# A hybrid layer kernel: attention without a loop and with two accumulators, early first loads, and a product of the delta layer on GpSimd

## The chip, the cores and the metric

The kernel runs on one core of a Trainium2 chip. The metric is the device time of one execution in microseconds, the median over several runs. A profiled execution gives the busy times, waits and timelines that are quoted here.

## What is computed

Four layers are added to a residual x of 4 x 1024 tokens and 128 channels: attention a, a mixture of experts, a gated delta layer b, and the same mixture of experts again. Cut to what matters here:

```python
# attention a, 16 heads of 8 channels
cov  = einsum('bhqd,bhkd->bhqk', q - mean(q), k - mean(k)) / d
attn = softmax(cov + q_var * k_var / d)
x    = x + (attn @ v) @ Wo.T
# delta layer b, per batch and head, state S of 8x8, over time t
S_new = a_t*S - a_t*b_t*(S k_t) k_t' + b_t * v_t k_t'
o_t   = q_t S_new
x     = x + O @ Wo.T + bo
```

## The kernel before, in words

The kernel is a chain of blocks in the order of `build`; each block gives every engine its own program, and engines meet through semaphores.

**Projection** (`project_qkv`, lines 264 to 433). The tokens go through in eight chunks of 512. TensorE projects q, k and v, ScalarE and VectorE split q and k into three bf16 parts, and SP stores these parts and those of the variances to DRAM (`scr.terms`, lines 424 and 428), four DMAs a chunk. The buffers of parts alternate between two. GpSimd clears the operand tiles `g.q_op` and `g.k_op` first (lines 311 and 315).

**Attention** (`attend`, from line 443). A unit is one batch and one group of four heads; there are 16 units, numbered u = 4b + s. SP loads the operands of a group, 3 DMAs for k and 9 for q, with `load` (lines 524 and 528). TensorE makes two kinds of score. Those for the maxima (line 567) are reduced by VectorE (line 696) over 1024 keys. The maxima are turned (line 621), split in three parts (lines 707 to 714), and written as rows of the operand. Those for the probabilities (line 582) come out transposed with the maxima already taken off; ScalarE takes their exponential (line 684). TensorE multiplies the exponentials with v into `ps_acc` (line 599). A unit has 32 steps. In a step TensorE issues two halves of maximum scores for a later unit, two probability scores and one product with v, all written out in this order in `body`. Both kinds of score have two PSUM buffers. After each half of the queries (16 steps) the accumulator is handed over: ScalarE copies `ps_acc` to SBUF in two parts (line 667, at places 7 and 8 of the exponentials, `COPY_AT`), TensorE turns the copy with four products against the identity (line 611) into `ps_misc`, and VectorE normalises from there (lines 719 and 725, one reciprocal and four multiplications). As there is one `ps_acc`, the product with v skips a step at the hand-over, and two are made in the next. `ps_misc` also takes the turned maxima. `batches` makes batch 0 and batch 3 straight code and runs batches 1 and 2 in a loop, on every engine. Groups of v are staged by GpSimd (line 511), one copy a unit.

The output projection, the expert layer, a convolution and the solve of the delta layer follow.

**Output part of the delta layer** (`delta_out`, from line 1861). For each of four batches and eight rows e of the state: TensorE spreads k (line 1934), VectorE multiplies it with u (line 2008), scans over time (line 2029) and multiplies the states with q (line 2035), and TensorE adds the result up (line 1944). The tiles `kd`, `St` and `qS` have two buffers each. After row 3, VectorE also adds the previous batch's output to x and takes its statistics (line 2015, `add`). GpSimd has only clearing to do in this block.

## Time and profile before

| | |
|---|---|
| median of three runs | 2043.8 us (2043.46 to 2047.93) |
| profiled execution | 2043.38 us, its span 2041.7 us |
| projection | 21 to 92 us |
| attention | 92 to 912 us |
| output projection, experts | 913 to 1160 us |
| delta layer's output part | 1633 to 1815 us |
| experts again | 1815 to 2041.7 us |
| VectorE busy | 1540.1 us (75%) |
| TensorE matmul busy | 1361.8 us (67%) |
| ScalarE busy | 917.1 us (45%) |
| GpSimd busy | 227.3 us (11%) |

Times in a timeline count from the start of the span. Busy time of matmuls is modelled: matmuls overlap, so the distance from one start to the next tells the pace, and the length of one does not. A line of a timeline may merge several instructions of one kind (x4). The words behind a left arrow name what ended the idle time before the instruction. PEclk is the share of full clock that TensorE was granted.

### The profile page before, as it was taken

To read this page: it belongs to the slowest core of one execution; us is meant where nothing else is said; L and a number is where in the kernel's file an instruction comes from. 1 tells how busy PE (TensorE), PEld (TensorE's weight loads), DVE (VectorE), ACT (ScalarE), POOL (GpSimd) and SP (SyncE) were. 2 spreads that over 40 slices of the span, in tenths; PEclk is the share of its full clock that TensorE was granted. 3 is DMA by queue.
4 is the path that set the end of the run, shared out by engine and by line. 5 is a ranking of instruction groups with operands and counts; after the bars stand their busy time and mean duration, and the time that the engine had idled before them with its cause. 6 is when DMAs were issued, how large, how long until landed. Compare 5 with 4: busy or idle time off the path is not lost. (4 is left out here: it accounts for less than half of the span.)

```text
span 2041.7 us, 44670 instructions
## 1 busy us (share of the span) xinstructions
PE 1361.8 (67%) x15216; PEld 723.2 (35%) x15216; DVE 1540.1 (75%) x3117; ACT 917.1 (45%) x2009; POOL 227.3 (11%) x218
## 2 busy tenths in 40 slices
PE   4489999999999999984399674000000078841998
PEld 2214444444444444443166442000000024420665
DVE  5598888888788888707166576899999899972665
ACT  4507777777677777774143273001222200030343
POOL 6000000000000000003414300000000000025044
PEclk9858999999999999997699876555555589965999
DMA  3430111111111110003224415810222010012243
GB/s 98 120 80 5 40 41 30 29 29 29 30 29 29 29 29 3 3 20 96 60 55 66 75 67 117 212 41 10 63 63 54 19 41 0 0 43 58 55 67 44
DMA packets 118670, 101.05 MB, mean 49 GB/s; under 512 B 23665, under 2 KB 100018, under 8 KB 118066
## 3 DMA queue, kind: packets, MB, share of 16 engines
q1 hardware_dynamic: 101570, 84.79, 16.2%
q0 software_dynamic: 11264, 8.92, 3.0%
q10 hardware_dynamic: 5616, 4.47, 1.3%
q8 instruction: 130, 2.13, 0.4%
q14 instruction: 90, 0.74, 0.1%
HBM read 55.98 MB, written 31.21 MB: 43 GB/s over the span
## 5 line engine op out<-in xcount | busy, mean ns | idle before, releaser
L696 DVE TENSOR_REDUCE att_negmax<-att_ps_max 128x1 f32<-128x1024 f32 x512 | 613.9, 1221 | 112.5 <-PE att_ps_max L567 91.8
L684 ACT ACTIVATE att_probs<-att_ps_prob 128x512 f32<-128x512 f32 x1024 | 561.4, 598 | 244.7 <-PE att_ps_prob L582 233.8
L567 PE MATMUL att_ps_max<-av_k_op,av_q_op 81*32 81x512 bf16 x4096 | 418.0, 404 | 43.1 <-DMA av_q_op<-terms_q 18.9
L582 PE MATMUL att_ps_prob<-av_q_op,av_k_op 99*32 99x512 bf16 x4096 | 406.9, 385 | 9.2 <-ACT att_probs L684 1.2
L599 PE MATMUL att_ps_acc<-att_probs,att_vq 128*32 128x256 f32 x4096 | 308.3, 381 | 0.0
L1926 PE MATMUL out_ps_y<-all_bo_row,all_ones 1*128 1x128 f32 x2 | 0.8, 482 | 372.8 <-PEq L104 372.8
L567 PEld LDWEIGHTS att_ps_max<-av_k_op,av_q_op 81*32 81x32 bf16 x4096 | 109.4, 98 | 184.2 <-DVE att_negmax L696 80.6
L582 PEld LDWEIGHTS att_ps_prob<-av_q_op,av_k_op 99*32 99x32 bf16 x4096 | 108.1, 95 | 174.1 <-ACT att_probs L684 129.7
L599 PEld LDWEIGHTS att_ps_acc<-att_probs,att_vq 128*32 128x32 f32 x4096 | 126.4, 111 | 82.3 <-issue 5.8
L1145 ACT ACTIVATE moe_moe_gate<-moe_moe_ps_h 128x256 f32<-128x256 f32 x122 | 46.8, 383 | 214.2 <-PE moe_moe_ps_h L1086 214.2
L1926 PEld LDWEIGHTS out_ps_y<-all_bo_row,all_ones 1*128 1x128 f32 x2 | 0.5, 305 | 373.1 <-issue 373.1
L1086 PE MATMUL moe_moe_ps_h<-all_w_all,moe_moe_xgT 128*128 x244 | 128.0, 607 | 1.4 <-DVE moe_moe_xgT L1286 1.4
L1310 DVE TENSOR_TENSOR moe_moe_y<-moe_moe_y,moe_moe_ps_y 128x128 f32 x182 | 52.4, 288 | 89.3 <-issue 81.0
L1835 ACT ACTIVATE solve_p<-solve_state,solve_decay 128x32 f32<-128x32 f32 x128 | 45.0, 351 | 155.7 <-DVE solve_state L1819 155.7
L1101 PE MATMUL moe_moe_ps_y<-all_w_all,moe_moe_hT 128*128 x728 | 111.6, 276 | 0.3
L1101 PEld LDWEIGHTS moe_moe_ps_y<-all_w_all,moe_moe_hT 128*128 128x128 f32 x728 | 95.7, 192 | 1.5 <-issue 1.5
L1286 DVE COPY moe_moe_xgT<-moe_moe_ps_g 128x256 f32<-128x256 f32 x92 | 38.2, 415 | 69.4 <-PE moe_moe_ps_g L1079 69.4
L511 POOL COPY att_vq<-av_v 128x288 f32<-128x288 f32 (+1 forms) x16 | 6.8, 427 | 728.6 <-PE att_ps_acc L599 728.5
L1079 PE MATMUL moe_moe_ps_g<-all_ident,moe_moe_xin 128*128 128x128 f32 x182 | 36.5, 280 | 69.8 <-DMA moe_moe_xin<-expert_rows 69.6
L1944 PE MATMUL out_ps_o<-out_qS,out_gather 128*128 128x512 f32 x128 | 65.0, 632 | 25.8 <-DVE out_qS L2035 25.7
L1302 DVE SCALAR_TENSOR_TENSOR moe_moe_hs<-moe_moe_gate,moe_moe_scale,moe_moe_ps_h 128x256 f32<-128x256 f32 x122 | 58.3, 478 | 20.2 <-ACT moe_moe_gate L1145 20.0
L2029 DVE TENSOR_TENSOR_SCAN out_St<-b_a,out_kd 128x1024 f32<-128x1024 f32 x32 | 73.1, 2284 | 0.4
(277 smaller groups left out, 2067.4 us busy)
## 6 DMA issues: line engine op xcount, KB each, us to landing
moe_moe_xin<-expert_rows SPq DMA_DIRECT2D x182, 72.0 KB, 1.8
av_k_op<-terms_k SPq DMA_DIRECT2D x48, 216.0 KB
av_q_op<-terms_q SPq DMA_DIRECT2D x144, 72.0 KB
solve_dec_and_windows<-solve_Xw SPq DMA_DIRECT2D x16, 256.0 KB, 3.0
solve_dec_and_windows<-solve_k SPq DMA_DIRECT2D x16, 256.0 KB, 3.7
terms_q<-qkv_parts_q SPq DMA_DIRECT2D x8, 384.0 KB, 2.6
terms_k<-qkv_parts_k SPq DMA_DIRECT2D x8, 384.0 KB, 3.2
all_w_all<-in_f_w SPq DMA_DIRECT2D x24, 128.0 KB, 2.5
```

The costliest lines, as they stand in the source:

```text
L567: mm = pe.matmul(ps_max[c * STRIP:(c + 1) * STRIP, a % 2, k * CH:(k + 1) * CH], q_op[s][0:R_ALL, h, at:at + STRIP], k_op[s][0:R_ALL, h, k ...
L582: mm = pe.matmul(ps_prob[c * STRIP:(c + 1) * STRIP, j % 2, :], k_op[s][0:R_END, h, at:at + STRIP], q_op[s][0:R_END, h, half * CH:(half + 1 ...
L599: mm = pe.matmul(ps_acc[32 * h:32 * h + 32, cols], vq[:, s % 2, kt, VW * h:VW * h + 32], probs[:, (GH * v + h) % PROBS, cols], start=(kt = ...
L684: act.activation(probs[:, j % PROBS, :], ps_prob[:, j % 2, :], ACT.Exp).then_inc(s_exp, 1)
L696: dve.tensor_reduce(negmax[:, s % 2, a:a + 1], ps_max[:, a % 2, :], AX.X, ALU.max, negate=True).then_inc(s_maxed, 1)
L1086: pe.matmul(ps_up[n % 3][:, :, :].rearrange("p w f -> p (w f)"), xgT[:, n // 2 % 3, cols], wall[:, bass.ds(at0, 2 * F)], start=True, stop= ...
L1101: mm = pe.matmul(ps_y[n % 2][:, 0:P], hT[:, n % 3, i * P:(i + 1) * P], wall[:, bass.ds(at0 + (2 * F + i * P), P)], start=(i == 0), stop=(i ...
L1145: act.activation(gate[:, n % 3, :], ps_up[n % 3][:, 0, :], ACT.Silu).then_inc(s_silu, 1)
L1302: dve.scalar_tensor_tensor(out=hs[:, n % 3, :], in0=gate[:, n % 3, :], scalar=scale[:, n:n + 1], in1=ps_up[n % 3][:, 1, :], op0=ALU.mult, ...
L1310: dve.tensor_tensor(tile, tile, ps_y[n % 2][:, 0:P], ALU.add).then_inc(s_sum, 1)
L1944: mm = pe.matmul(ps_o[:, i * CH:(i + 1) * CH], gather[:, e, :, :].rearrange("p h d -> p (h d)"), qS[:, e % 2, i * CH:(i + 1) * CH], start= ...
L2029: dve.tensor_tensor_scan(St[:, e % 2, :], a[:, tok], kd[:, e % 2, :], 0.0, ALU.mult, ALU.add).then_inc(s_S, 1)
```

## The change

Four things are changed.

1. The operands of the first two head groups of batch 0 are loaded by SP inside the projection, two sets (of one DMA for k and three for q) after each of the chunks 2, 3 and 4, once the first two chunks are stored and the operand tiles cleared. The loop over chunks on SP is written out.
2. All four batches of attention are straight code on every engine.
3. There are two accumulators in PSUM, one for each half of the queries, and no `ps_misc`. The copied accumulator is turned by four transposes back into its own accumulator's bank, and VectorE normalises from there with one reciprocal and one multiplication. The turned maxima go to the first accumulator. The product with v comes in every step. It waits at the start of a half for the last reader of that bank, and no longer for the copy of the other half. The copies come at places 6 and 8.
4. In the delta layer's output part the product of q with the states is made by GpSimd. VectorE's scan waits for the product two before.

```diff
@@ -416,25 +416,48 @@
 
         @block.sync
         def _(sp):
-            def body(i):
-                for p in range(2):
-                    at = (2 * i + p) * CH
-                    for w in range(2):
-                        sp.wait_ge(s_p3[w][p], i + 1)
-                        sp.dma_start(scr.terms[w][:, 0:D, :, bass.ds(at, CH)].rearrange("i d h t -> (d h) i t"),
-                                     parts[w][:, p, :, :]).then_inc(s_out[p], 16)
-                    sp.wait_ge(s_v3[p], i + 1)
-                    for w in range(2):
-                        sp.dma_start(scr.terms[w][:, D, :, bass.ds(at, CH)].rearrange("i h t -> h i t"),
-                                     vparts[32 * w:32 * w + H, p, :, :]).then_inc(s_out[p], 16)
-            repeat(sp, NC_ // 2, body)
+            def store(c):
+                i, p = c // 2, c % 2
+                tok = slice(c * CH, (c + 1) * CH)
+                for w in range(2):
+                    sp.wait_ge(s_p3[w][p], i + 1)
+                    sp.dma_start(scr.terms[w][:, 0:D, :, tok].rearrange("i d h t -> (d h) i t"),
+                                 parts[w][:, p, :, :]).then_inc(s_out[p], 16)
+                sp.wait_ge(s_v3[p], i + 1)
+                for w in range(2):
+                    sp.dma_start(scr.terms[w][:, D, :, tok].rearrange("i h t -> h i t"),
+                                 vparts[32 * w:32 * w + H, p, :, :]).then_inc(s_out[p], 16)
+
+            early = [(s, i) for s in range(EARLY) for i in range(NPART)]
+            for c in range(NC_):
+                store(c)
+                if c == 2:
+                    for p in range(2):
+                        sp.wait_ge(s_out[p], 16 * NDMA)
+                    sp.wait_ge(s_ones, 1 + 3 * NQ)
+                if c >= 2:
+                    for s, i in early[2 * (c - 2):2 * (c - 1)]:
+                        load_terms(sp, g, scr, 0, s, i)
             for p in range(2):
                 sp.wait_ge(s_out[p], 16 * NDMA * (NC_ // 2))
 
 
+EARLY = 2
+
+
+def load_terms(sp, g, scr, b, s, i):
+
+    heads, tok, row = slice(s * GH, (s + 1) * GH), slice(b * S, (b + 1) * S), i * NPART * K1
+    sp.dma_start(g.k_op[s][row:row + NPART * K1, :, :],
+                 scr.terms[1][:, :, heads, tok].rearrange("j d h t -> (j d) h t")).then_inc(g.s_load[s], 16)
+    for j in range(NPART):
+        sp.dma_start(g.q_op[s][row + j * K1:row + (j + 1) * K1, :, :],
+                     scr.terms[0][i, :, heads, tok]).then_inc(g.s_load[s], 16)
+
+
 LEAD = 8
 PV_LAG = 3
-COPY_AT = 2 * PV_LAG + 1
+COPY_AT = 2 * PV_LAG
 PROBS = 16
 STEPS = GH * TB
...
-        ps_acc = m.ps("ps_acc", [P, CH])
-        ps_misc = m.ps("ps_misc", [P, CH])
-        comb = ps_misc[:, P:P + CT * GH * VW].rearrange("p (t g r) -> p t g r", t=CT, g=GH)
...
-        def batches(eng, body):
-
-            body(0, True, False)
-            with eng.Fori(1, last_b) as b:
-                body(b, False, False)
-            body(last_b, False, True)
+        def batches(body):
+
...
-                                 ).then_inc(s_load[s], 16)
-                    for j in range(NPART):
-                        sp.dma_start(q_op[s][row + j * K1:row + (j + 1) * K1, :, :],
-                                     scr.terms[0][i, :, heads, tok]).then_inc(s_load[s], 16)
+                    load_terms(sp, g, scr, b, s, i)
 
...
-            for s in range(NQ):
+            for s in range(EARLY, NQ):
                 load(0, s)
...
-                        pe.wait_ge(s_acc, 2 * u + half)
+                    if kt == 0:
+                        read = max(1, 3 * u) if half == 0 else 3 * u + 1
+                        pe.wait_ge(s_misc, read)
 
                 for h in range(GH):
-                    mm = pe.matmul(ps_acc[32 * h:32 * h + 32, cols], vq[:, s % 2, kt, VW * h:VW * h + 32],
+                    mm = pe.matmul(ps_acc[half][32 * h:32 * h + 32, cols], vq[:, s % 2, kt, VW * h:VW * h + 32],
                                    probs[:, (GH * v + h) % PROBS, cols], start=(kt == 0 and part == 0),
                                    stop=(kt == TB - 1 and part == 1))
                 mm.then_inc(s_pv, 1)
 
-            def combine(b, s, half, last=False):
+            def combine(b, s, half):
 
                 u = NQ * b + s
                 pe.wait_ge(s_acc, 2 * u + half + 1)
-
-                pe.wait_ge(s_misc, 3 * u + 1 + 2 * half - last)
                 for t in range(CT):
-                    mm = pe.matmul(comb[:, t], acc_sb[:, half, t * P:(t + 1) * P],
-                                   g.ident[:, :].rearrange("p (g r) -> p g r", g=GH)[:, :, 0:VW],
-                                   start=True, stop=True)
+                    mm = pe.transpose(ps_acc[half][:, t * P:(t + 1) * P], acc_sb[:, half, t * P:(t + 1) * P],
+                                      g.ident[:, :])
                 mm.then_inc(s_comb, 1)
 
             def turn_max(b, s):
                 u = NQ * b + s
                 pe.wait_ge(s_maxed, STEPS * (u + 1))
-                if not (isinstance(b, int) and b == 0 and s == 0):
+                if not (b == 0 and s == 0):
                     pe.wait_ge(s_misc, 3 * u - 1)
-                pe.transpose(ps_misc[0:STEPS, 0:P], negmax[:, s % 2, :], g.ident[:, :]).then_inc(s_nmT, 1)
+                pe.transpose(ps_acc[0][0:STEPS, 0:P], negmax[:, s % 2, :], g.ident[:, :]).then_inc(s_nmT, 1)
 
             for a in range(STEPS):
...
                             scores_for_prob(b, s, 2 * i + half)
                         w = i - PV_LAG
-
-                        for w in (w - 1, w) if w % (2 * TB) == 1 else () if w % (2 * TB) == 0 else (w,):
-                            if w >= 0:
-                                pv(b, s, w // 2, w % 2)
-                            elif not (first and s == 0):
-                                pv(*prev(b, s), (w + STEPS) // 2, w % 2)
+                        if w >= 0:
+                            pv(b, s, w // 2, w % 2)
+                        elif not (first and s == 0):
+                            pv(*prev(b, s), (w + STEPS) // 2, w % 2)
                         if i == PV_LAG + 1 and not (first and s == 0):
                             combine(*prev(b, s), 1)
                         if i == STEPS // 2 + PV_LAG + 1:
                             combine(b, s, 0)
                         if i == STEPS - LEAD + 1 and not (last and s == NQ - 1):
                             turn_max(*nxt(b, s, 1))
-            batches(pe, body)
+            batches(body)
             for w in range(STEPS - PV_LAG, STEPS):
                 pv(last_b, NQ - 1, w // 2, w % 2)
-            combine(last_b, NQ - 1, 1, last=True)
+            combine(last_b, NQ - 1, 1)
 
         @block.scalar
         def _(act):
...
-                    if not (isinstance(b, int) and b == 0 and s == 0):
+                    if not (b == 0 and s == 0):
                         act.wait_ge(s_comb, 2 * u + half - 1)
                 cols = slice(part * CH // 2, (part + 1) * CH // 2)
-                ins = act.activation(acc_sb[:, half, cols], ps_acc[:, cols], ACT.Copy)
+                ins = act.activation(acc_sb[:, half, cols], ps_acc[half][:, cols], ACT.Copy)
                 if part == 1:
                     ins.then_inc(s_acc, 1)
...
-                            copy_acc(*prev(b, s), 1, j - COPY_AT)
-                        if STEPS + COPY_AT <= j <= STEPS + COPY_AT + 1:
-                            copy_acc(b, s, 0, j - STEPS - COPY_AT)
+                        if j in (COPY_AT, COPY_AT + 2) and not (first and s == 0):
+                            copy_acc(*prev(b, s), 1, (j - COPY_AT) // 2)
+                        if j in (STEPS + COPY_AT, STEPS + COPY_AT + 2):
+                            copy_acc(b, s, 0, (j - STEPS - COPY_AT) // 2)
                         act.wait_ge(s_prob, 2 * STEPS * u + j + 1)
                         if j % GH == 0 and not (first and s == 0 and j < PROBS):
 
                             act.wait_ge(s_pv, 4 * TB * u + 2 * ((j - PROBS) // GH + 1))
                         act.activation(probs[:, j % PROBS, :], ps_prob[:, j % 2, :], ACT.Exp).then_inc(s_exp, 1)
-            batches(act, body)
...
                 chain.done(dve.tensor_copy(parts[:, 0, :], rows))
                 chain.done(dve.tensor_tensor(rest, rows, parts[:, 0, :], ALU.subtract))
...
-                dve.reciprocal(rsum[:, half, :, :], comb[:, :, :, D]).then_inc(s_rsum, 1)
+                dve.reciprocal(rsum[:, half, :, :], comb[half][:, :, :, D]).then_inc(s_rsum, 1)
                 dve.wait_ge(s_rsum, 2 * u + half + 1)
-                for t in range(CT):
-                    tile = b * TB + half * CT + t
-                    out = g.o[:, bass.ds(tile, 1), s * GH * D:(s + 1) * GH * D].rearrange(
-                        "p o (g d) -> p (o g) d", g=GH)
-                    ins = dve.tensor_tensor(out, comb[:, t, :, 0:D],
-                                            rsum[:, half, t, :].unsqueeze(2).to_broadcast([P, GH, D]), ALU.mult)
-                ins.then_inc(s_misc, 1)
+                tile = b * TB + half * CT
+                out = g.o[:, tile:tile + CT, s * GH * D:(s + 1) * GH * D].rearrange("p t (g d) -> p t g d", g=GH)
+                dve.tensor_tensor(out, comb[half][:, :, :, 0:D],
+                                  rsum[:, half, :, :].unsqueeze(3).to_broadcast([P, CT, GH, D]),
+                                  ALU.mult).then_inc(s_misc, 1)
 
             for a in range(STEPS):
...
@@ -1921,6 +1925,14 @@
             pool.wait_ge(s_same, 3)
             pool.memset(gather[:, :, :, :], 0.0).then_inc(s_same, 1)
 
+            for b in range(B):
+                for e in range(D):
+                    n = D * b + e
+                    pool.wait_ge(s_S, n + 1)
+                    wait_used(pool, s_o, n - 1)
+                    pool.tensor_tensor(qS[:, e % 2, :], q[:, b * S:(b + 1) * S], St[:, e % 2, :],
+                                       ALU.mult).then_inc(s_qS, 1)
+
         @block.tensor
         def _(pe):
             pe.matmul(ps_y[0][:, 0, :], g.ones[0:1, :], g.bo_row[:, :], start=True, stop=True).then_inc(s_bo, 1)
@@ -2020,22 +2032,20 @@
                 for t in range(TB):
                     bn_stats_of(nc, g, b * TB + t)
 
-            def body(b):
-                tok = bass.ds(b * S, S)
+            for b in range(B):
+                tok = slice(b * S, (b + 1) * S)
                 spread_u(b, 0)
                 for e in range(D):
                     n = D * b + e
                     dve.wait_ge(s_kd, n + 1)
+                    wait_used(dve, s_qS, n - 1)
                     dve.tensor_tensor_scan(St[:, e % 2, :], a[:, tok], kd[:, e % 2, :], 0.0, ALU.mult,
                                            ALU.add).then_inc(s_S, 1)
                     if e < D - 1:
+                        dve.wait_ge(s_S, n)
                         spread_u(b, e + 1)
-                    dve.wait_ge(s_S, n + 1)
-                    wait_used(dve, s_o, n - 1)
-                    dve.tensor_tensor(qS[:, e % 2, :], q[:, tok], St[:, e % 2, :], ALU.mult).then_inc(s_qS, 1)
-                    if e == 3 and not (isinstance(b, int) and b == 0):
+                    if e == 3 and b:
                         add(b - 1)
-            repeat(dve, B, body)
             add(B - 1)
 
         @block.scalar
```

## Rows read from the trace of the kernel before

**Rows 1.** Busy time by stretch: stretch, length, then busy us per engine, PEclk, DMA.
```profile
253.00:300.00 47.00, 45.85 (x797) 22.64 (x788) 40.84 (x49) 35.72 (x69) 0.43 (x1) 1.00 0.14 32
```

**Rows 2.** Timeline of GpSimd in attention: start us, length us, engine, line, operation.
```profile
206.94 0.43 POOL L511 COPY att_vq<-av_v 128x288 f32<-128x288 f32 x1 [112.77 <-PE att_ps_acc L599]
...
347.72 0.43 POOL L511 COPY att_vq<-av_v 128x288 f32 x1 [46.46 <-PE att_ps_acc L599]
...
734.41 0.43 POOL L511 COPY att_vq<-av_v 128x288 f32<-128x288 f32 x1 [47.14 <-PE att_ps_acc L599]
...
828.24 0.43 POOL L511 COPY att_vq<-av_v 128x288 f32<-128x288 f32 x1 [46.49 <-PE att_ps_acc L599]
```

**Rows 3.** Timeline of TensorE matmuls round one hand-over of the accumulator.
```profile
300.42 0.39 PE L567 MATMUL att_ps_max<-av_k_op,av_q_op 81*32 81x512 bf16 x4
...
303.87 1.08 PE L611 MATMUL att_ps_misc<-all_ident,att_acc_sb 128*128 128x36 f32 x8
...
304.88 0.40 PE L567 MATMUL att_ps_max<-av_k_op,av_q_op 81*32 81x512 bf16 x4
...
306.19 0.39 PE L567 MATMUL att_ps_max<-av_k_op,av_q_op 81*32 81x512 bf16 x4
```

**Rows 4.** Timeline of TensorE in the output projection: four transposes, then the next four.
```profile
923.81 0.60 PE L809 MATMUL oproj_ps_t<-all_ident,a_o 128*128 128x128 f32 x4
...
924.25 0.60 PE L824 MATMUL oproj_ps_x<-all_ident,all_x 128*128 128x128 f32 x4
```

**Rows 5.** Timeline of ScalarE in attention: an accumulator copy, a pair of exponentials.
```profile
302.31 0.41 ACT L667 ACTIVATE att_acc_sb<-att_ps_acc 128x256 f32<-128x256 f32 x1
...
308.16 1.09 ACT L684 ACTIVATE att_probs<-att_ps_prob 128x512 f32<-128x512 f32 x2 [0.22 <-PE att_ps_prob L582]
```

**Rows 6.** Timeline of all engines, from the projection to the first score.
```profile
37.15 14.20 POOL L315 MEMSET av_k_op<- 3x4096 bf16 x4
...
51.48 0.39 SPq L428 DMA_DIRECT2D terms_k<-qkv_vparts  x1
...
92.25 0.29 SPq L524 DMA_DIRECT2D av_k_op<-terms_k  x1
...
103.80 1.90 PE L567 MATMUL att_ps_max<-av_k_op,av_q_op 81*32 81x512 bf16 x16 [18.86 <-DMA av_q_op<-terms_q]
```

**Rows 7.** Busy time by stretch: the delta layer's output part.
```profile
1645.00:1803.00 158.00, 131.82 (x373) 60.37 (x371) 154.34 (x144) 7.27 (x16) 0.00 (x0) 0.98 0.00 0
```

**Rows 8.** Timeline of VectorE in the delta layer's output part.
```profile
1645.51 1.22 DVE L2008 TENSOR_TENSOR out_kd<-out_u,out_ps_k 128x1024 f32<-128x1024 f32 x1 [3.97 <-PE out_ps_k L1934]
...
1646.76 2.29 DVE L2029 TENSOR_TENSOR_SCAN out_St<-b_a,out_kd 128x1024 f32<-128x1024 f32 x1
...
1664.56 2.28 DVE L2029 TENSOR_TENSOR_SCAN out_St<-b_a,out_kd 128x1024 f32<-128x1024 f32 x1
...
1666.77 1.19 DVE L2008 TENSOR_TENSOR out_kd<-out_u,out_ps_k 128x1024 f32<-128x1024 f32 x1
...
1669.01 2.28 DVE L2029 TENSOR_TENSOR_SCAN out_St<-b_a,out_kd 128x1024 f32<-128x1024 f32 x1
...
1799.61 1.23 DVE L2035 TENSOR_TENSOR out_qS<-b_q,out_St 128x1024 f32<-128x1024 f32 x1
```

**Rows 9.** GpSimd's groups by line and shape: busy us, mean ns, idle before.
```profile
L511 POOL COPY att_vq<-av_v 128x288 f32<-128x288 f32 x8 | 3.4, 427 | 346.3 <-PE att_ps_acc L599 346.2
```

**Rows 10.** Timeline of VectorE and of GpSimd at the start of the expert layer.
```profile
957.37 1.08 DVE L1241 TENSOR_TENSOR moe_moe_lower<-moe_moe_base,moe_moe_first 128x896 f32<-128x896 f32 x1
...
957.90 1.60 POOL L1055 DMA_INDIRECT expert_rows<-moe_moe_xr,moe_moe_slot  x1 [11.30 <-ACT moe_moe_xr L1135]
...
962.83 0.97 POOL L1055 DMA_INDIRECT expert_rows<-moe_moe_xr,moe_moe_slot  x1 [0.30 <-issue]
...
964.03 0.69 DVE L1251 TENSOR_TENSOR_SCAN moe_moe_upto<-moe_moe_unit,moe_moe_needed 128x256 f32<-128x256 f32 x1
...
964.10 1.39 POOL L1055 DMA_INDIRECT expert_rows<-moe_moe_xr,moe_moe_slot  x1 [0.30 <-issue]
```

More of the change, by code:

```diff
@@ L461, in attend @@
         ps_prob = m.ps("ps_prob", [P, 2, CH])
-        ps_acc = m.ps("ps_acc", [P, CH])
-        ps_misc = m.ps("ps_misc", [P, CH])
-        comb = ps_misc[:, P:P + CT * GH * VW].rearrange("p (t g r) -> p t g r", t=CT, g=GH)
+        ps_acc = [m.ps(f"ps_acc{half}", [P, CH]) for half in range(2)]
+        comb = [a[:, :].rearrange("p (t g r) -> p t g r", t=CT, g=GH) for a in ps_acc]
         s_clear = m.sem("cleared")
-        s_load = m.sems("loaded", NQ)
         s_scored = m.sem("scored")
@@ L577, in scores_for_prob @@
                     pe.wait_ge(s_nmrow, 16 * NPART * (u + 1))
-                if not (isinstance(b, int) and b == 0 and s == 0 and j < 2):
+                if not (b == 0 and s == 0 and j < 2):
                     pe.wait_ge(s_exp, 2 * STEPS * u + j - 1)
@@ L693, in reduce_max @@
                 dve.wait_ge(s_scored, STEPS * u + a + 1)
-                if a == 0 and not (isinstance(b, int) and b == 0 and s < 2):
+                if a == 0 and not (b == 0 and s < 2):
                     dve.wait_ge(s_nmT, u - 1)
@@ L702, in split_max @@
                 dve.wait_ge(s_nmT, u + 1)
-                if not (isinstance(b, int) and b == 0 and s < 2):
+                if not (b == 0 and s < 2):
                     dve.wait_ge(s_nmrow, 16 * NPART * (u - 1))
@@ L706, in split_max @@
                 rows, rest, parts = nm_rows[:, :], nm_rest[:, :], nm_parts[:, s % 2]
-                ins = dve.tensor_copy(rows, ps_misc[0:STEPS, 0:P])
+                ins = dve.tensor_copy(rows, ps_acc[0][0:STEPS, 0:P])
                 ins.then_inc(s_misc, 1)
-                dve.wait_ge(s_misc, 1 if isinstance(u, int) and u == 0 else 3 * u)
+                dve.wait_ge(s_misc, max(1, 3 * u))
                 chain.done(dve.tensor_copy(parts[:, 0, :], rows))
@@ L2021, in add @@
                     bn_stats_of(nc, g, b * TB + t)
-            def body(b):
-                tok = bass.ds(b * S, S)
+            for b in range(B):
+                tok = slice(b * S, (b + 1) * S)
                 spread_u(b, 0)
```

19 lines of the change are left out of this document (8 added, 11 removed).

## The prediction

> **What bounds the kernel now.** I read the busy time by stretch first, then the timelines of GpSimd, of TensorE and of VectorE where the change reaches. One attention unit (a batch and a group of four heads, of which there are 16) has TensorE busy for 45.85 of 47.0 us at granted clock 1.00, and VectorE for 40.84 [rows 1]. So TensorE is the bound there, and VectorE is close enough to stop it at times. The copies of v on GpSimd mark the units, since each waits for the products of an earlier unit: three static units take 140.78 us (46.93 each), the two last 93.83 us (46.92 each), but the eight intervals that touch the loop take 386.69 us (48.34 each) [rows 2]. Inside a unit an ordinary step of TensorE takes 304.88 to 306.19, 1.31 us, while the two steps from 300.42 to 304.88, in which the accumulator changes hands, take 4.46 us: 1.84 us beyond two ordinary steps, of which 1.01 is the combining product [rows 3]. In the output part of the delta layer VectorE is busy for 154.34 of 158.0 us and TensorE for 131.82 [rows 7]. There VectorE is the bound, one step (products with k, scan, product with q) taking 1664.56 to 1669.01, 4.45 us [rows 8].
>
> **Part 1, early loads.** The first score waits until 103.80, though the attention block's queue starts at 92.25 [rows 6]. The change issues the operands of head groups 0 and 1 in the projection, 2 load sets (8 DMAs) after each of chunks 2, 3 and 4. SP is moved past two things. One is the wait for GpSimd's memsets, which end at 37.15 + 14.20 = 51.35, before chunk 2's last store is issued at 51.48 [rows 6], so I cost it at nothing. The other is the stores of chunks 3 to 5, each queued behind 8 issues of 0.3 to 0.4 us (the block's first is 0.29), some 3 us of a chunk of 8 (eight chunks from 21 to 92 us, less the first one's start); what hides this is that parts buffers are wanted again only two chunks later, and if the cover goes, up to 3 us for each of three chunks are lost. TensorE can begin some 0.02 us behind the block's first issue, so the gain is 103.80 - 92.27 = **11.5 us**. What is late next is VectorE's own chain of maxima, which simply starts earlier; groups 2 and 3 are still loaded in the block and are not wanted for over 50 us.
>
> **Part 2, no loop in attention.** All four batches become straight code for all five engines. Batches 0 and 3 are already that, so their pace is the measure: 386.69 - 8 x 46.92 = **11.3 us**. The bounds of this term are 0 (if the longer code has to be fetched at a cost that batches 0 and 3 don't show) and 11.3; I take 11.3, since the static rows are the same code.
>
> **Part 3, the hand-over of the accumulator.** There are 31 hand-overs that something waits for: one in the first unit, two in each of the fifteen others (the very last counts below). Three things shrink each. The combining product becomes four transposes; the nearest rows have four transposes 128x128 f32 issued in 923.81 to 924.25, 0.44 us [rows 4], in place of 1.01. Two PSUM buffers take away the reason for skipping one step of the probability-value product and doing two in the next. The ScalarE copies go to places 6 and 8 of the exponentials instead of 7 and 8; each takes 0.4 us, and a pair of exponentials 1.09 [rows 5], so two steps ask 1.5 us of ScalarE where TensorE has 1.31 and then 1.31 plus the transposes. I work out that the second exponential of the first such step ends at 1.9 us from that step's start, and TensorE wants its buffer at 1.96 less a latency of some 0.2: a wait of 0.1 to 0.2, plus 0.1 on switching to the transposes. New excess: 0.44 + 0.3 = 0.75 against 1.84, a gain of 1.09 x 31 = **33.8 us**. Bounds: 1.4 each (0.44 alone, 43 us) and 0.57 each (only the shorter combine, 18 us). The added waits on the readers of the PSUM buffers (normalise, split of the maxima) stand three or more steps behind those readers and cost nothing; if they did, scores and products queued behind them on TensorE, and ScalarE after them, would stop. Normalise becomes one multiplication instead of four; it mostly overlaps, and with the shorter end of the last unit I give it **2 us**. Attention together: 11.5 + 11.3 + 33.8 + 2 = **58.6 us less**.
>
> **Part 4, the product with q on GpSimd.** It takes 1.23 us from each of 32 steps of VectorE [rows 8] and adds 32 products of 128x1024 on GpSimd, with a wait for the scan ahead of each, and a wait of each scan for the product two before. Behind GpSimd's wait nothing else is queued; who waits for it is TensorE's sum and, two steps on, the scan. No row shows such a product. The nearest is a one-input copy of 288 columns in 0.427 us [rows 9]; with 0.1 for the start that is 1.15 ns a column, so 1024 columns take 1.3 us if a second input is free and 2.4 to 2.5 if it costs as much as the first. I take 2.3, near the upper end, because both inputs have to be read. The Trainium skill (GPSIMD Engine Reference, section 3.1) gives 4497 ns for 2048 columns of a two-input add; half of it, 2.25, would change the sum by 1.6 us.
>
> Whether this overlaps the scan decides the part. The trace has GpSimd instructions that read SBUF while VectorE works. Behind a VectorE multiply or scan with two SBUF inputs they last longer: 1.60 us, begun 0.55 us before such an instruction ended, and 1.39 us, begun just as a scan started; between the two, with no such instruction beside it, one takes 0.97 [rows 10]. So GpSimd is held while such a VectorE instruction runs, and the scan is one. Then in each step scan and product exclude one another: 2.28 + 0.1 (semaphore) + 2.3 + 0.1 (release) = 4.78 us, in place of 4.45. This holds whichever of the two yields. The rows show only GpSimd yielding. The Trainium skill (SBUF — State Buffer, section Who interferes with whom) says the first to start keeps the shared ports for its whole instruction and the other blocks fully, either way round; no row shows the reverse. By that rule and its 2.25 the part would cost some 6 us, and with no such rule it would gain 21.
>
> Sum for the stage, from the first product at 1645.51. Before: it ends at 1799.61 + 1.23, 155.3 us. That is 1.25 (1645.51 to 1646.76) + 31 x 4.45 + three adds + the last scan and product, 3.5, and leaves 4.2 us for each add. After: 1.25 + 31 x 4.78 = 149.4; three adds at 4.2 less the 1.3 us that VectorE now idles in a step, 8.7; the last scan and product 4.7; together 162.8. So **7.5 us more**. The vector engine's saving of 39 us goes into its wait for GpSimd.
>
> **The sum.** The profiled execution took 2043.4 us (span 2041.7 and 1.7 around it), 0.4 under the median of 2043.8. 2043.4 - 58.6 + 7.5 = 1992.3; I forecast **1992.5 us**.
>
> **Rivals.**
> (a) Scan and product overlap. Then VectorE's step is 1.25 + 2.21 (1664.56 to 1666.77) = 3.45 us and it needs 1.25 + 31 x 3.45 + 12.6 + 4.7 = 125.5 us and TensorE, with 131.8 busy [rows 7] and little idle left, becomes the bound at about 134: 21 us less instead of 7.5 more, in all 2043.4 - 58.6 - 21 = **1964 us**. For it: the delayed GpSimd rows are DMA issues, not arithmetic. Against it: their delays follow the ends of the two-input VectorE instructions.
> (b) The hand-over gains only the shorter combine, because ScalarE's copies or VectorE's split of the maxima become what TensorE waits for (VectorE has 40.84 of 47.0 us already [rows 1]): 33.8 falls to 18, **2008 us**. For it: only two buffers lie between each pair of engines.
> (c) The change doesn't do what it says: the loads don't land early, or they hold up the stores, and the 11.5 us come back: **2004 us**. Against it: DMA has room between the stores.
> (d) Slower than before: GpSimd's product is far slower than the copy's rate says. Every 1 us beyond 2.3 costs 32 us, so from about 3.9 us a product (2.3 + 51/32) the whole is slower; at 4.5 us it is 1992.3 + 70 = **2063 us**. Against it: that would be 3.8 times the copy's time for a column.
>
> **Chances.** Forecast 0.66, (a) 0.19, (b) 0.07, (c) 0.04, (d) 0.04. A measurement of this kernel can tell about 0.2% (4 us) from no change. Faster by over that: all but (d) and a sliver, 0.95; within it 0.01; slower 0.04. The range reaches down past (a) to 1960, since a fifth lies there, and up to 2003, for a product of 2.46 us (5 more) and part of (b). Around the forecast alone it would be 1982 to 2001.
>
> **What would show it.** First score at about 92.3. Units of 44.7 us, all alike, with hand-overs of 3.3 to 3.4 us for two steps, and no idle gap of TensorE in mid-attention. In the delta output, scans 4.8 us apart with VectorE idle 1.3 us in each step, released by GpSimd, and GpSimd busy nearly half of the stage with products that begin at a scan's end. Scans about 4 us apart and TensorE without gaps would prove (a); a product that starts and goes on while a scan runs, both at their lengths, disproves the exclusion. A product over 3 us, units above 46 us, or a first score after 100 us would make the forecast wrong.

## The result and the profile after

The changed kernel takes 1984.35 us (median of four runs, 1981.33 to 1986.57); the kernel before 2043.63 us (2041.33 to 2047.93). The ratio is 0.9707, with a 95% interval of 0.9685 to 0.9728. The profiled execution took 1985.79 us, its span 1984.1 us, which is 57.6 us less than the one of before.

Where these 57.6 us went, by the starts of the blocks: attention ends 62.4 us earlier (the expert layer starts at 876.42 instead of 938.80). From there to the delta layer's output part it takes 697.3 us instead of 694.5, and the last expert layer 228.6 instead of 226.6. Nothing is changed in these two stretches; in the other kernels below, where they are the same code, they take 693.8 to 700.6 and 226.0 to 227.7, so I count the 4.8 us as scatter, though 228.6 lies 0.9 us above what any other kernel shows. The output part takes 181.80 us instead of 181.78.

**Attention.** First the start, in the timelines of SP's queue and of TensorE (start, duration, engine, line, operation, output <- input, count; in brackets the idle time before and what ended it):

```profile
51.82 0.43 SPq L428 DMA_DIRECT2D terms_k<-qkv_vparts  x1
52.37 0.27 SPq L451 DMA_DIRECT2D av_k_op<-terms_k  x1
52.68 1.06 SPq L454 DMA_DIRECT2D av_q_op<-terms_q  x3
...
70.70 1.00 SPq L454 DMA_DIRECT2D av_q_op<-terms_q  x3
```
```profile
92.72 1.90 PE L577 MATMUL att_ps_max<-av_k_op,av_q_op 81*32 81x512 bf16 x16 [7.23 <-PEq L104]
```

The first score starts at 92.72 instead of 103.80 [rows 6], and it no longer waits for a DMA (PEq is TensorE's own sequencer). Then the units, by GpSimd's copies of v, where the loop used to be:

```profile
415.65 0.43 POOL L530 COPY att_vq<-av_v 128x288 f32<-128x288 f32 x1 [44.09 <-PE att_ps_acc L610]
460.24 0.43 POOL L530 COPY att_vq<-av_v 128x288 f32<-128x288 f32 x1 [44.16 <-PE att_ps_acc L610]
504.79 0.43 POOL L530 COPY att_vq<-av_v 128x288 f32<-128x288 f32 x1 [44.12 <-PE att_ps_acc L610]
549.37 0.43 POOL L530 COPY att_vq<-av_v 128x288 f32<-128x288 f32 x1 [44.16 <-PE att_ps_acc L610]
```

All 13 intervals are 44.50 to 44.65 us, where [rows 2] had 46.92 outside of the loop and 48.34 at it. One hand-over on TensorE:

```profile
482.38 0.65 PE L610 MATMUL att_ps_acc<-att_probs,att_vq 128*32 128x256 f32 x8
482.81 0.43 PE L577 MATMUL att_ps_max<-av_k_op,av_q_op 81*32 81x512 bf16 x4
483.03 0.44 PE L592 MATMUL att_ps_prob<-av_q_op,av_k_op 99*32 99x512 bf16 x4
483.25 0.44 PE L577 MATMUL att_ps_max<-av_k_op,av_q_op 81*32 81x512 bf16 x4
483.47 0.44 PE L592 MATMUL att_ps_prob<-av_q_op,av_k_op 99*32 99x512 bf16 x4
483.70 0.65 PE L610 MATMUL att_ps_acc<-att_probs,att_vq 128*32 128x256 f32 x8
484.28 0.66 PE L620 MATMUL att_ps_acc<-all_ident,att_acc_sb 128*128 128x128 f32 x4
484.87 0.40 PE L577 MATMUL att_ps_max<-av_k_op,av_q_op 81*32 81x512 bf16 x4
```

An ordinary step is 1.31 us; this one is 482.81 to 484.87, 2.06, so the excess is 0.75 instead of 1.84 [rows 3]. The transposes are issued 0.15 us later than the pace would have them (484.28 instead of 484.13), and the next score 0.59 behind them.

**The delta layer's output part.** Timelines of VectorE and GpSimd, and the groups of the block (count | busy us, mean ns | idle before and its releaser):

```profile
1593.96 1.19 DVE L2020 TENSOR_TENSOR out_kd<-out_u,out_ps_k 128x1024 f32<-128x1024 f32 x1
1595.18 3.44 DVE L2042 TENSOR_TENSOR_SCAN out_St<-b_a,out_kd 128x1024 f32<-128x1024 f32 x1
1598.54 1.19 DVE L2020 TENSOR_TENSOR out_kd<-out_u,out_ps_k 128x1024 f32<-128x1024 f32 x1
1599.77 3.44 DVE L2042 TENSOR_TENSOR_SCAN out_St<-b_a,out_kd 128x1024 f32<-128x1024 f32 x1
...
1594.12 2.35 POOL L1933 TENSOR_TENSOR out_qS<-b_q,out_St 128x1024 f32<-128x1024 f32 x1 [2.23 <-DVE out_St L2042]
1598.70 2.36 POOL L1933 TENSOR_TENSOR out_qS<-b_q,out_St 128x1024 f32<-128x1024 f32 x1 [2.23 <-DVE out_St L2042]
```
```profile
L2042 DVE TENSOR_TENSOR_SCAN out_St<-b_a,out_kd 128x1024 f32<-128x1024 f32 x32 | 105.2, 3288 | 1.0
L2020 DVE TENSOR_TENSOR out_kd<-out_u,out_ps_k 128x1024 f32<-128x1024 f32 x32 | 38.1, 1191 | 4.0 <-PE out_ps_k L1946 4.0
...
L1933 POOL TENSOR_TENSOR out_qS<-b_q,out_St 128x1024 f32<-128x1024 f32 x32 | 75.3, 2353 | 90.1 <-DVE out_St L2042 90.1
```

The product takes 2.353 us. The scan, 2.28 us before [rows 8], is now recorded with a mean of 3.288: 28 of the 32 take some 3.44, and the first of all and the one behind each of the three `add`, which have no product beside them, take 2.27 to 2.29. The one shown begins at 1595.18, while the product of 1594.12 runs (until 1596.47), and ends at 1598.62, 2.15 us behind the product's end. The next product starts 0.08 us later. A step is 4.58 us. The product with k (1598.54 to 1599.73) has one input in PSUM, lies beside a product on GpSimd (from 1598.70), and neither is longer for it. VectorE is busy by the records nearly as long as before and has hardly any idle time: its wait is inside the scan.

### The profile page after: what moved, and what is told of

It reads as the page before. It is cut to its first block and busy times, and to the rows that moved or that the text cites. A ratio compares the mean times of both kernels' runs of the same rounds, so it can differ in the third digit from the quotient of the medians.

```text
span 1984.1 us, 42351 instructions
## 1 busy us (share of the span) xinstructions
PE 1330.6 (67%) x15088; PEld 724.9 (37%) x15088; DVE 1533.5 (77%) x2989; ACT 916.6 (46%) x2009; POOL 302.3 (15%) x250
## 5 line engine op out<-in xcount | busy, mean ns | idle before, releaser
L577 PE MATMUL att_ps_max<-av_k_op,av_q_op 81*32 81x512 bf16 x4096 | 420.5, 401 | 24.4 <-DVE att_negmax L702 15.5
L610 PE MATMUL att_ps_acc<-att_probs,att_vq 128*32 128x256 f32 x4096 | 314.8, 379 | 0.0
L577 PEld LDWEIGHTS att_ps_max<-av_k_op,av_q_op 81*32 81x32 bf16 x4096 | 114.5, 97 | 160.5 <-DVE att_negmax L702 62.8
L610 PEld LDWEIGHTS att_ps_acc<-att_probs,att_vq 128*32 128x32 f32 x4096 | 133.3, 111 | 76.5 <-issue 0.5
L530 POOL COPY att_vq<-av_v 128x288 f32<-128x288 f32 x16 | 6.8, 427 | 672.0 <-PE att_ps_acc L610 671.9
L2042 DVE TENSOR_TENSOR_SCAN out_St<-b_a,out_kd 128x1024 f32<-128x1024 f32 x32 | 105.2, 3288 | 1.0
L1933 POOL TENSOR_TENSOR out_qS<-b_q,out_St 128x1024 f32<-128x1024 f32 x32 | 75.3, 2353 | 90.1 <-DVE out_St L2042 90.1
```

The lines of the kernel that those rows point to most:

```text
L577: mm = pe.matmul(ps_max[c * STRIP:(c + 1) * STRIP, a % 2, k * CH:(k + 1) * CH], q_op[s][0:R_ALL, h, at:at + STRIP], k_op[s][0:R_ALL, h, k ...
L610: mm = pe.matmul(ps_acc[half][32 * h:32 * h + 32, cols], vq[:, s % 2, kt, VW * h:VW * h + 32], probs[:, (GH * v + h) % PROBS, cols], start ...
L1933: pool.tensor_tensor(qS[:, e % 2, :], q[:, b * S:(b + 1) * S], St[:, e % 2, :], ALU.mult).then_inc(s_qS, 1)
L2042: dve.tensor_tensor_scan(St[:, e % 2, :], a[:, tok], kd[:, e % 2, :], 0.0, ALU.mult, ALU.add).then_inc(s_S, 1)
```

## The experiments

The experiments ran in three rounds on three chips, each beside the kernel before, which took 2043.77 to 2045.55 us there. The ratios allow for that; of two times from different rounds, a difference of 2 us says nothing, as the kernel before alone moved by 1.8.

### Product back on VectorE

```diff
-                    pool.tensor_tensor(qS[:, e % 2, :], q[:, b * S:(b + 1) * S], St[:, e % 2, :],
-                                       ALU.mult).then_inc(s_qS, 1)
...
-                    wait_used(dve, s_qS, n - 1)
...
+                    dve.wait_ge(s_S, n + 1)
+                    wait_used(dve, s_o, n - 1)
+                    dve.tensor_tensor(qS[:, e % 2, :], q[:, tok], St[:, e % 2, :], ALU.mult).then_inc(s_qS, 1)
```

> The changed kernel with the product of q with the states back on VectorE, everything else as changed. If the product on GpSimd and the scan exclude one another (a step of 4.58 us in place of 4.45, but 1.2 us less behind each add), the output part takes 155 us either way and the whole stays at 1984, within 3 us. If the product on GpSimd had cost the 7.5 us that was forecast, this kernel would take 1977. If it had gained anything by overlap, this kernel would take more than 1990.

Measured: 1981.94 us, ratio to before 0.9695 (0.9679 to 0.9711), against 0.9707 (0.9685 to 0.9728) with the product on GpSimd. The block takes 181.2 us, a step 4.45. So moving the product is worth nothing that can be measured: the intervals overlap, the block differs by 0.6 us, and the 59 us come from attention.

### The scan's second input from PSUM

```diff
-                wait_used(pe, s_kd, n - 1)
+                wait_used(pe, s_S, n - 1)
...
-                dve.tensor_tensor(kd[:, e % 2, :], u[:, bass.ds(b * S, S)], ps_k[e % 2][:, :],
+                dve.tensor_tensor(ps_k[e % 2][:, :], u[:, bass.ds(b * S, S)], ps_k[e % 2][:, :],
...
-                    dve.tensor_tensor_scan(St[:, e % 2, :], a[:, tok], kd[:, e % 2, :], 0.0, ALU.mult,
+                    dve.tensor_tensor_scan(St[:, e % 2, :], a[:, tok], ps_k[e % 2][:, :], 0.0, ALU.mult,
```

> The changed kernel with the products u times k written back into their PSUM tile, so that the scan has one input in SBUF and one in PSUM; TensorE waits for the scan before it overwrites the tile. Exclusion by the two SBUF inputs: scan and product run beside one another, the scan is recorded at 2.3 us again, a step falls from 4.58 to 3.5 to 4.1 us with TensorE as the bound, the output part from 155 to about 134 us, the whole to about 1963. Exclusion of any VectorE work by GpSimd, or a cost of the waits alone: the step stays at 4.5 us or more and the whole at 1984.

Measured: 1961.88 us (1958.44 to 1962.68), ratio to before 0.959 (0.9574 to 0.9606), 22.5 us below the changed kernel and 20.1 below the product on VectorE. The block takes 157.4 us, 24.4 less than in the changed kernel. Its timelines of VectorE and GpSimd:

```profile
1593.15 2.29 DVE L2041 TENSOR_TENSOR_SCAN out_St<-b_a,out_ps_k 128x1024 f32<-128x1024 f32 x1
1595.36 1.21 DVE L2019 TENSOR_TENSOR out_ps_k<-out_u,out_ps_k 128x1024 f32<-128x1024 f32 x1
1596.60 2.29 DVE L2041 TENSOR_TENSOR_SCAN out_St<-b_a,out_ps_k 128x1024 f32<-128x1024 f32 x1
...
1595.52 2.35 POOL L1932 TENSOR_TENSOR out_qS<-b_q,out_St 128x1024 f32<-128x1024 f32 x1 [1.09 <-DVE out_St L2041]
```

The product runs from 1595.52 to 1597.87 and the scan starts in the middle of it, at 1596.60; both have their own length. A step is 3.45 us. This is what rival (a) of the prediction described, and its 1964 us is 2 us off. It had TensorE as the bound at 134 us; in fact VectorE sets most steps, and waits for TensorE's products with k for 10.7 us in all, 4.0 in the changed kernel. Only the place of one tile has changed, which the product with k writes and the scan reads, and with it what TensorE waits for before it overwrites that tile. The product with k ran free beside GpSimd already when it wrote to SBUF, so the exclusion belongs to the scan with two SBUF inputs.

### The control: the same scan, product on VectorE

The diff is that of the two experiments above, taken together.

> A control for the experiment in which the scan reads its second input from PSUM: the same scan and the same PSUM buffer, but the product with q on VectorE as in the kernel before. If that experiment's gain came from overlap with GpSimd alone, a step takes 1.17 + 2.28 + 1.23 less the overlaps of one instruction's start with the one before = 4.45 us as before and the time is 1983 us, within 3. If reading from PSUM makes the scan or the product with k faster by itself, the step is below 4.3 us and the time below 1979 us.

Measured: 1985.20 us, ratio 0.9717 (0.9698 to 0.9736), a step again 4.45 us with the scan at 2.280. PSUM makes nothing faster by itself. The 20 to 24 us need both: the product on GpSimd, and a scan that leaves GpSimd alone.

### The product made twice

GpSimd makes each product twice; nobody reads the first.

```diff
+                    pool.tensor_tensor(qS[:, 2 + e % 2, :], q[:, b * S:(b + 1) * S], St[:, e % 2, :], ALU.mult)
                     pool.tensor_tensor(qS[:, e % 2, :], q[:, b * S:(b + 1) * S], St[:, e % 2, :],
```

> The changed kernel with each product on GpSimd made twice, the first into a tile that nobody reads. Exclusion: a step becomes 2.23 + 2 x 2.35 = 6.9 us, the output part 31 x 2.35 + 2 = 75 us longer, the whole about 2059. If scan and product may overlap and only GpSimd's own time counts, a step is 4.8 us and the whole about 1991.

Measured: one run of 2043.38 us; the block takes 242.1 us, 60 more, and a step 6.60. Far from what overlap would give, but 16 us below the 2059 that I wrote. The timelines of VectorE and GpSimd say why:

```profile
1602.32 4.36 DVE L2043 TENSOR_TENSOR_SCAN out_St<-b_a,out_kd 128x1024 f32<-128x1024 f32 x1
...
1602.18 2.35 POOL L1933 TENSOR_TENSOR out_qS<-b_q,out_St 128x1024 f32<-128x1024 f32 x1
1604.49 4.33 POOL L1934 TENSOR_TENSOR out_qS<-b_q,out_St 128x1024 f32<-128x1024 f32 x1
1608.78 2.35 POOL L1933 TENSOR_TENSOR out_qS<-b_q,out_St 128x1024 f32<-128x1024 f32 x1
```

The scan waits from 1602.32 for the first product, which ends at 1604.53. It goes before the second product, and ends at 1606.68, 2.15 us later. The second product, recorded from 1604.49, ends 2.14 us after the scan. So here GpSimd is held by VectorE, and one of its instructions is recorded at 4.33 us instead of 2.35. The exclusion works in both directions, and a scan that waits goes in between two products that are both ready. Only the head of a held instruction is free: the second product costs 2.14 us, not 2.35, and 31 x (6.60 - 4.58) is 63 us. The block shows 60; 4 of the 32 second products were not held, and I did not follow the last 3 us further.

### Three buffers for the states and the products

```diff
-        St = m.sb("St", [P, 2, S])
-        qS = m.sb("qS", [P, 2, S])
+        St = m.sb("St", [P, 3, S])
+        qS = m.sb("qS", [P, 3, S])
...
-                    wait_used(dve, s_qS, n - 1)
-                    dve.tensor_tensor_scan(St[:, e % 2, :], a[:, tok], kd[:, e % 2, :], 0.0, ALU.mult,
+                    wait_used(dve, s_qS, n - 2)
+                    dve.tensor_tensor_scan(St[:, n % 3, :], a[:, tok], kd[:, e % 2, :], 0.0, ALU.mult,
```

> The changed kernel with three buffers for the states and for their products with q in place of two, and the waits one buffer further back. Exclusion: nothing changes, 4.58 us a step and 1984. If the scan had been held by the wait for the product two before, a step falls to 3.5 to 4.1 us and the whole to about 1963.

Measured: one run of 1985.36 us, the scan still 3.43 us long and 4.58 from the next. The scan's wait is no wait for a buffer.

### The loop of the kernel before, written out

```diff
-            body(0, True, False)
-            with eng.Fori(1, last_b) as b:
-                body(b, False, False)
-            body(last_b, False, True)
+            for b in range(B):
+                body(b, b == 0, b == last_b)
```

> The kernel before with all four batches of attention as straight code and nothing else changed. My theory: all units take 46.9 us, 11.3 us less in all, 2032.3. If long straight code has to be fetched at a cost, the gain is smaller or gone, 2036 to 2044. No change of the second unit after the loop's turn would mean that the 7.6 us there belong to something else.

Measured: 2033.40 us, ratio 0.9939 (0.9915 to 0.9962). The 13 intervals are 46.91 to 46.98 us, 610.2 in all instead of 621.3, so 11.1 us of pace. Two of them, by the copies of v:

```profile
442.55 0.43 POOL L509 COPY att_vq<-av_v 128x288 f32<-128x288 f32 x1 [46.54 <-PE att_ps_acc L597]
489.53 0.43 POOL L509 COPY att_vq<-av_v 128x288 f32<-128x288 f32 x1 [46.55 <-PE att_ps_acc L597]
```

What a turn of the loop cost is in the trace of before: TensorE's waits from 340 to 740 us, and its busy time and granted clock in the stretch of the turn beside the one ahead of it (us, busy of PE, PEld, DVE, ACT, POOL, PEclk, DMA share, GB/s).

```profile
PE att_ps_max L567 <- issue: 3.6, 1, 3.6
```
```profile
480.00:535.00 55.00, 50.90 (x877) 25.43 (x869) 47.41 (x55) 39.97 (x76) 0.43 (x1) 1.00 0.12 30
535.00:560.00 25.00, 22.60 (x332) 10.59 (x336) 16.17 (x18) 14.87 (x28) 0.43 (x1) 0.86 0.21 52
```

There was one idle stretch of 3.6 us without a releaser, at 533 to 537, and a granted clock of 0.86 over the 25 us around it. Cut finer, the clock falls behind the idle stretch:

```profile
533.00:537.00 4.00, 0.36 (x12) 0.02 (x4) 0.96 (x1) 0.61 (x2) 0.00 (x0) 0.96 0.47 101
537.00:540.00 3.00, 3.00 (x32) 1.30 (x36) 1.22 (x1) 1.19 (x2) 0.00 (x0) 0.50 0.59 151
540.00:543.00 3.00, 3.00 (x36) 1.22 (x32) 1.23 (x1) 1.20 (x2) 0.00 (x0) 0.50 0.59 142
543.00:546.00 3.00, 2.95 (x48) 1.03 (x40) 2.28 (x2) 2.45 (x6) 0.43 (x1) 0.92 0.13 36
```

TensorE had been busy at 1.00, stood idle for 3.6 us, and then worked at 0.50, the lower level of 1.2 GHz, for some 6.8 us by these rows, which costs 3.4 us (an estimate: half of them). The interval with the turn was 54.5 us instead of 46.9, 7.6 more: 3.6 for the idle stretch, 3.4 for the clock, and 0.6. The other seven were 47.2 to 47.9, 0.3 to 0.9 us more than outside the loop, with no single gap.

### The early loads taken out

```diff
-EARLY = 2
+EARLY = 0
```

> The changed kernel with all first loads in the attention block again. Theory: the first score comes at 104 in place of 92.7 and the whole is 11 us longer, 1995.5. If the start of attention were covered by something else, or the early loads cost the projection, it would be less than 8.

Measured: 1998.77 us, ratio 0.977 (0.9744 to 0.9796), 14.4 above the changed kernel. TensorE's first score:

```profile
105.30 1.90 PE L577 MATMUL att_ps_max<-av_k_op,av_q_op 81*32 81x512 bf16 x16 [19.20 <-DMA av_q_op<-terms_q]
```

It is 12.6 us later than with early loads, and attention ends 13.8 us later. I had expected 11 us. The same first score came at 103.80 before and at 104.86 in the kernel without the loop, so this start scatters by some 1.5 us, and the loads are worth 11 to 14 us.

### The hand-over, one thing at a time

Four kernels undo parts of the hand-over. The first has the four products against the identity again:

```diff
-                    mm = pe.transpose(ps_acc[half][:, t * P:(t + 1) * P], acc_sb[:, half, t * P:(t + 1) * P],
-                                      g.ident[:, :])
+                    mm = pe.matmul(comb[half][:, t, :, 0:VW], acc_sb[:, half, t * P:(t + 1) * P],
+                                   g.ident[:, :].rearrange("p (g r) -> p g r", g=GH)[:, :, 0:VW],
+                                   start=True, stop=True)
```

> The changed kernel with the copied accumulator turned by four products with 36 columns of the identity, as before, in place of four transposes. Theory: each hand-over is 0.57 us longer for TensorE, 32 of them, 18 us more, 2002. If TensorE is held by ScalarE or VectorE at the hand-over anyway, the transposes are hidden and the time rises by less than 8.

The second has the copies at places 7 and 8 (`COPY_AT = 2 * PV_LAG + 1`, and the second copy at `COPY_AT + 1`):

> The changed kernel with ScalarE's two copies ahead of exponentials 7 and 8 in place of 6 and 8. My working gave the place of the copies 0.1 to 0.2 us of a hand-over; at 7 and 8 the second exponential of the first step and the first of the next are both late, so 0.1 to 0.3 us more for each of 31 hand-overs, 3 to 9 us in all, 1987 to 1993. If the place is nothing, 1984.

The third has the skipped and doubled step of the product with v:

```diff
-                        if w >= 0:
-                            pv(b, s, w // 2, w % 2)
+                        for w in (w - 1, w) if w % (2 * TB) == 1 else () if w % (2 * TB) == 0 else (w,):
+                            if w >= 0:
+                                pv(b, s, w // 2, w % 2)
```

> The changed kernel with one thing of part 3 undone: the product with v again skips its step at a hand-over and two are made in the next. Two accumulators, transposes and places 6 and 8 stay. The kernel after spends 44.55 us on a unit and the kernel before, with its loop unrolled, 46.95, so a hand-over gained 1.2 us; the runs so far attribute 0.41 of it to the transposes and 0.12 to the places of the copies, and leave 0.67. Theory A: the rest is the order: with the skip, TensorE issues in one step the combining product behind two products with v, and the scores for ScalarE and VectorE come late. Then units are about 45.9 us and the time 1985 + 21 = 2006 us. Theory B: the three things overlap and none is worth much alone (each is hidden by what the others leave), then units are below 45.1 us and the time is below 1994 us.

The fourth has all three, so that of the hand-over only the two accumulators and the shorter normalise are left:

> The changed kernel with the order of the product with v, the combining product (four products against the identity) and the places of the copies all as before; of part 3 there remain only the two accumulators in PSUM and the shorter normalise. If the gain is in these three (theory A), the units are as before, about 46.9 us, and the time is 1985 + 31 x 1.15 = 2021 us. If two banks are worth something by themselves (theory B: TensorE need not wait for the copy of the old accumulator before the next product), the units stay below 46.5 us and the time is below 2014 us.

Measured, with the mean of the 13 intervals as the unit:

| kernel | us (ratio, 95% interval) | unit, us | beyond after, per hand-over |
|---|---|---|---|
| after | 1984.35 (0.9707, 0.9685 to 0.9728) | 44.56 | |
| copies at 7 and 8 | 1988.16 (0.9713, 0.969 to 0.9736) | 44.80 | 0.12 |
| product skips | 1996.25 (0.9765, 0.9748 to 0.9781) | 45.09 | 0.27 |
| products, no transposes | 1997.12 (0.9763, 0.9743 to 0.9784) | 45.37 | 0.41 |
| all three | 2012.62 (0.9844, 0.9828 to 0.9861) | 46.46 | 0.95 |
| before, loop written out | 2033.40 (0.9939, 0.9915 to 0.9962) | 46.94 | 1.19 |

One interval each, with the product skipping and with all three:

```profile
465.14 0.43 POOL L530 COPY att_vq<-av_v 128x288 f32<-128x288 f32 x1 [44.66 <-PE att_ps_acc L610]
510.25 0.43 POOL L530 COPY att_vq<-av_v 128x288 f32<-128x288 f32 x1 [44.67 <-PE att_ps_acc L610]
```
```profile
428.25 0.43 POOL L530 COPY att_vq<-av_v 128x288 f32<-128x288 f32 x1 [46.04 <-PE att_ps_acc L610]
474.69 0.43 POOL L530 COPY att_vq<-av_v 128x288 f32<-128x288 f32 x1 [46.01 <-PE att_ps_acc L610]
```

Of 1.19 us, 0.41 are the transposes, 0.27 the order, 0.12 the copies' places; undone together the three cost 0.95, 0.15 more than one by one. The last 0.24 belong to what this kernel still has, two accumulators and the shorter normalise. No run parts them, but the traces show where most of it lies: in twelve hand-overs of the kernel without the loop the doubled product with v starts 0.37 us behind the last score, in twelve of this one 0.22 to 0.23. With two accumulators this product no longer waits for the copy of the old one, so I put these 0.14 us to them; no run shows it alone. With the four products I had expected 18 us more, at 0.57 a hand-over, and got 13, at 0.41. One hand-over of that kernel in TensorE's timeline:

```profile
490.63 0.61 PE L610 MATMUL att_ps_acc<-att_probs,att_vq 128*32 128x256 f32 x8
491.17 1.08 PE L620 MATMUL att_ps_acc<-all_ident,att_acc_sb 128*128 128x36 f32 x8
492.18 0.40 PE L577 MATMUL att_ps_max<-av_k_op,av_q_op 81*32 81x512 bf16 x4
```

The products hold TensorE's issue for 1.01 us (491.17 to 492.18), the transposes for 0.59 (484.28 to 484.87). The copies' places came out as expected: with 7 and 8 one score of the step starts 0.33 to 0.37 us behind the one before in nearly all of twelve hand-overs, instead of 0.22.

Before the last two runs I had put 0.67 on the order (theory A: units of 45.9 us, 2006 us); it is 0.27. Theory B wanted units below 45.1 and a time below 1994: the units are 45.09, the time 1996.25, so it is met on the pace and missed on the time. And of the fourth kernel I had written that the units would be as before (46.9) or below 46.5 if two banks are worth something by themselves: 46.46 is just on that side. Its median is 8 us below the 2021 of the first theory.

## Why the prediction was right, step by step

**The whole.** I forecast 1992.5 us; it is 1984.35. The direction and the mechanism of each part held. Two terms of the sum were off: the hand-over too small, by most of the 3.8 us that attention gained beyond 58.6, and the output part too dear, by 7.5. Together that is 11.3 us; 4.8 us of scatter in the unchanged stretches went the other way, and the median lies 1.4 us below the profiled execution. That the whole is only 8 us off is in part luck.

**Part 1.** Forecast 11.5 us from a first score at 92.27. It came at 92.72, 11.1 us earlier, and the kernel without early loads shows 11 to 14. The issues do not hold up the stores: the loads go out from 52.37 on, in the gaps between chunks, as costed at nothing.

**Part 2.** Forecast 11.3. The kernel before with the loop written out gained 11.1 us of pace and 10 to 12 us in all. The lower bound, code that has to be fetched, did not show.

**Part 3.** The mechanism held, the size of one term did not. On TensorE the hand-over read above has an excess of 0.75 us, as forecast to the hundredth, and that is luck: the inside differs. The four transposes hold the issue for 0.59 us, not 0.44 [rows 4] and 0.1 for the switch. The wait of 0.1 to 0.2 for ScalarE's second exponential is not there: in twelve hand-overs all scores of the step are issued at the pace of 0.22. In its place 0.10 to 0.16 pass ahead of the transposes, and 0.10 to 0.11 also ahead of the turned maxima, where no copy is near. But the unit fell by 46.94 - 44.56 = 2.38 us, 1.19 for each hand-over and not 1.09: I read one pair of steps [rows 3] and took it for the whole. 31 x 0.10 is 3.1 us. About half of it is a step some 4 us behind each hand-over of before that was 0.05 longer than its neighbours (0.92 instead of 0.87 us from its second half to the next step) and no longer is. Most of the rest is that 0.75 was one of the longer hand-overs after: the mean of twelve is 0.72. Attention in all gained 62.4 where I had 58.6: 11.1 and 11.1 for the first two parts, 31 x 1.19 = 36.9 here, and 3.3 left for the ends, for which I had 2. Of its steps, the share of the transposes (1.01 - 0.44 = 0.57) was too high, 0.41 by the run, and the order with its two banks made up for it. Rival (b), a gain of the shorter combine alone at 0.57 each, is out: two things other than the transposes are worth 0.39 apart and more together.

**Part 4.** The product: forecast 2.3 us, bounds 1.3 to 2.5, measured 2.353. The exclusion: right, and shown by the pair of kernels that differ in the scan's input. The Trainium skill (SBUF — State Buffer, section Who interferes with whom) has it both ways round, whoever starts first, which [rows 10] did not show. The trace agrees: a scan held by a product is recorded at 3.44 us instead of 2.28, a product held by a scan at 4.33 instead of 2.35. The failed term is the step, 2.28 + 0.1 + 2.3 + 0.1 = 4.78. It is 4.58: 2.35 for the product, 2.15 for the scan and 0.08 to hand over. I added the scan's full 2.28 and a release of 0.1, as if VectorE had started only when the product ended. In fact the scan is already issued and is held inside, so its head (2.28 - 2.15) and its wait's latency lie under the product. 31 x 0.20 is 6.2 us, and each `add` cost 2.5 us net instead of 2.9, 1.3 us for three. Together these are the 7.5 us that I forecast and that did not come: from the first product with k at 1585.91 to the last product's end at 1738.91 + 2.34 the stage takes 155.3 us, as before. The saving of 1.23 us in a step and the cost of the exclusion cancel almost exactly.

**Rivals.** (a) is refuted for this kernel and realised by the one with the PSUM operand. (c) and (d) are out, by the first score and by 2.353 us.

**What I had said the profile would show.** Right: the first score, units of 44.7 (44.56), the hand-over, GpSimd busy for nearly half of the stage (75.3 of 155), products that begin at a scan's end. Wrong in form: I expected VectorE idle for 1.3 us in a step, released by GpSimd. It shows no idle time but scans that are 1.15 us too long. Whoever looks only at idle times and waits sees VectorE as the bound there, 105.2 us of scans, and misses that 28 of the 32 stand still for a third of their length.

## What to carry to other kernels

Before work is moved from VectorE to GpSimd, look at which of VectorE's instructions beside it read two operands from SBUF: the time saved can come back as waiting inside them, as it did here in the scan, the only such instruction that was tried beside arithmetic on GpSimd. Leaving one of the operands in PSUM, where it already was, turned a move worth nothing into some 20 us. And an instruction's own mean duration, against the same form in the kernel before, belongs to the reading of a trace as much as the idle times.

## What the runs showed of the hardware

- A scan 128x1024 with two SBUF inputs and a GpSimd product with two SBUF inputs exclude one another in whole instructions; the one that waits is recorded as running (3.44 instead of 2.28 us, 4.33 instead of 2.35). With one of the scan's inputs in PSUM both keep their length (2.286 and 2.355 us) side by side.
- When GpSimd had two products ready and a scan of VectorE waited, the scan went in between: 28 of 32 second products were recorded at 4.33 us. The reverse, two such instructions ready on VectorE and one waiting on GpSimd, was not tried.
- The turn of the loop in attention cost an idle stretch of 3.6 us on TensorE and, with a granted clock of 0.50 for some 6.8 us behind it, 7.6 us in its interval, more than twice the gap itself.
